# Layer 1 of a graph network on one core: groups written out with constant waits, PSUM operands for DVE, and the next group's scores taken between the adds

## The reference

```
s_u = x @ W_u.T + b_u ;  s_v = x @ W_v.T
e = s_u[src] + s_v[dst];  e = where(e >= 0, e, 0.2 * e)
m = segment_max(e, dst);  e_exp = exp(e - m[dst])
denom = segment_sum(e_exp, dst);  probs = e_exp / denom[dst]
msg = x.reshape(n, 32, 8)[src] * probs[:, None, :]
out = segment_sum(msg, dst)
```

## Time and profile before

| | |
|---|---|
| median of 3 runs | 4665.82 us (4657.55 to 4666.35) |
| profiled execution: its time, its span | 4686.26 us, 4684.5 us |
| busy share of the span: POOL, PE, DVE, ACT | 74%, 66%, 47%, 19% |
| gathers of layer 1 (L1466), 880 | 1039.2 us busy, 326.9 us idle before them |
| products (L1701), 220 | 264.2 us, 1222 ns each |
| adds (L1611), 440 | 188.3 us, 428 ns each |
| matmuls of the pairs (L1532) | 553.5 us |
| mean granted clock of PE | 0.814 |

### The profile page before, as it was taken

How to read it: one execution, slowest core, us unless ns; L and a number is a source line. 1 busy time by engine, 2 the same in 40 slices (tenths; PEclk the granted TensorE clock), 3 DMA queues, 4 the chain that set the end, 5 groups by cost and what they waited for, 6 DMA issues and landing times. The chain is left out here.

```text
span 4684.5 us, 61408 instructions
## 1 busy us (share of the span) xinstructions
PE 3095.6 (66%) x13554; PEld 1900.7 (41%) x13555; DVE 2213.4 (47%) x5019; ACT 908.4 (19%) x2810; POOL 3468.7 (74%) x2948
## 2 busy tenths in 40 slices
PE   2548777877777777777777776884545555555541
PEld 1224444444444444444444443552333333443331
DVE  2553333333333333333333332995766667766665
ACT  0212222222222222222222222332000000000002
POOL 4237888888888888888888886775777777777764
PEclk9768888889888888888889897996777767667765
DMA  8667666667666667666667666565443434444431
GB/s 300 168 235 176 125 132 134 133 126 138 129 133 125 133 131 135 124 133 130 135 125 131 133 133 132 177 202 172 115 113 109 113 113 114 114 112 114 114 102 63
DMA packets 471759, 641.52 MB, mean 137 GB/s; under 512 B 173607, under 2 KB 365635, under 8 KB 467886
## 3 DMA queue, kind: packets, MB, share of 16 engines
q0 software_dynamic: 198144, 339.26, 38.1%
q1 hardware_dynamic: 245994, 254.83, 18.2%
q10 hardware_dynamic: 27588, 47.08, 3.1%
HBM read 448.23 MB, written 192.71 MB: 137 GB/s over the span
## 5 line engine op out<-in xcount | busy, mean ns | idle before, releaser
L935 POOL DMA_INDIRECT S<-l_msum,l_sink x784 | 1284.8, 1639 | 254.2 <-issue 213.0
L1466 POOL DMA_INDIRECT l_feats<-X_rows,l_gsrc x880 | 1039.2, 1181 | 326.9 <-issue 264.6
L918 POOL DMA_INDIRECT l_ga<-A_rows,l_gsrc x784 | 789.7, 1007 | 265.6 <-issue 160.0
L1008 PE MATMUL l_psU<-l_hid,l_same 128*128 128x257 f32 x1568 | 585.9, 459 | 535.6 <-ACT l_hid L1044 505.3
L981 PE MATMUL l_psC<-l_table,l_onehot 128*128 x4728 | 727.4, 295 | 0.0
L1532 PE MATMUL l_psU<-l_feats,l_same 128*128 128x264 f32 x1760 | 553.5, 478 | 169.5 <-DVE l_feats L1701 124.6
L1048 ACT COPY l_msum<-l_psU 128x257 f32<-128x257 f32 x784 | 292.6, 373 | 1889.9 <-POOLq L934 1313.6
L974 PE MATMUL l_psC<-W1cT,l_attrT 64*128 64x256 f32 x1576 | 623.4, 479 | 13.0 <-DMA l_table<-B_rows 13.0
L981 PEld LDWEIGHTS l_psC<-l_table,l_onehot 128*128 128x128 bf16 x4728 | 426.1, 104 | 367.9 <-issue 306.0
L1008 PEld LDWEIGHTS l_psU<-l_hid,l_same 128*128 128x128 f32 x1568 | 267.4, 214 | 666.2 <-ACT l_hid L1044 579.0
L1532 PEld LDWEIGHTS l_psU<-l_feats,l_same 128*128 128x128 f32 x1760 | 409.0, 240 | 306.9 <-issue 216.8
(11 more groups left out here) (346 smaller groups left out, 3390.7 us busy)
## 6 DMA issues: line engine op xcount, KB each, us to landing
l_srcb<-src_rows SPq DMA_DIRECT2D x99, 512.0 KB
l_locb<-lo_rows SPq DMA_DIRECT2D x55, 512.0 KB
S<-su_zeros ACTq DMA_DIRECT2D x24, 1156.5 KB
l_locb<-loc_rows SPq DMA_DIRECT2D x99, 256.0 KB
nd_sums<-S SPq DMA_DIRECT2D x196, 128.5 KB, 2.2
l_attr<-in_edge_attr SPq DMA_DIRECT2D x98, 256.0 KB
GH_rows<-l_hidden SPq DMA_DIRECT2D x49, 384.0 KB
nd_hidden<-GH_rows SPq DMA_DIRECT2D x49, 384.0 KB, 3.1
```

What stands on the lines that cost most here:

```text
L918: pool.indirect_dma_start(ga[:, s, :], None, D["A"], bass.IndirectOffsetOnAxis(ap=gsrc[h][:, j % HALF:j % HALF + 1], axis=0)).then_inc(gat ...
L935: pool.indirect_dma_start(D[f"S{j % NTAB}"], bass.IndirectOffsetOnAxis(ap=sink[j // HALF][:, j % HALF:j % HALF + 1], axis=0), msum[:, j % ...
L1008: nc.tensor.matmul(psU[j % 2][:, 0:UW], same[j // HALF][:, j % HALF, :], hid[:, j % RING, :], start=True, stop=True).then_inc(agg_done, 1)
L1466: pool.indirect_dma_start(feats[r][:, t, :], None, D["X1"], bass.IndirectOffsetOnAxis(ap=gsrc[r][:, t:t + 1], axis=0)).then_inc(gathered[r ...
```

## The change

It does five things, all in layer 1. All 55 groups are written out, on every engine, with constants in the waits in place of register values. A constant row of lane numbers is copied once into a new PSUM bank `psW`, and `find_edge` compares from there. ACT takes the exponential twice: first into `psW`, from where the four products read the weights, then into the gathered rows as before, where PE needs them for the denominators (`weights_in_rows`, for which PE now waits). DVE takes the next group's scores right behind the fourth product, then adds 4 and 5, the local maximum, and adds 6 and 7. PE turns the next group's scores between pairs 5 and 6.

```
+        psW = m.ps("psW", [P, 512])
+        weight = psW[:, 0:GROUP * NH].rearrange("p (t h) -> p t h", h=NH)
+        column = psW[:, P:2 * P]
         def groups(engine, body):
-            body(0, 0, True, False)
-            body(1, 1, False, False)
-            with engine.Fori(1, (XG - 3) // SETS) as u:
-                for r in range(SETS):
-                    body(u * SETS + r, r, False, False)
-            for g in range(XG - 3, XG):
-                body(g, g % SETS, False, g == XG - 1)
+            for g in range(XG):
+                body(g, g % SETS, g == 0, g == XG - 1)
         def ahead(engine, body):
-            with engine.Fori(0, (XG - SETS) // SETS) as u:
-                for r in range(SETS):
-                    body(u * SETS + r, r)
-            body(XG - SETS - 1, 0)
+            for g in range(XG - SETS):
+                body(g, g % SETS)
 # PE
                 pe.wait_ge(same_ready, g + 1)
+                pe.wait_ge(weights_in_rows, g + 1)
                 for n in range(PAIRS):
...
                     i.then_inc(agg_done, 1)
+                    if n == 5 and not last:
+                        turn_scores(g + 1, 1 - r)
                 if not last:
-                    turn_scores(g + 1, 1 - r)
                     gather_ends(g + 1)
 # ACT
                 act.wait_ge(below_ready, g + 1)
-                nc.scalar.activation(feats[r][:, :, H:XW], below[:, :, :], ACT.Exp).then_inc(weights_ready, 1)
+                nc.scalar.activation(weight, below[:, :, :], ACT.Exp).then_inc(weights_ready, 1)
+                nc.scalar.activation(feats[r][:, :, H:XW], below[:, :, :], ACT.Exp).then_inc(weights_in_rows, 1)
 # DVE
-                nc.vector.tensor_tensor(same[:, :, :], K["column"][:, :].unsqueeze(1).to_broadcast([P, GROUP, P]),
+                nc.vector.tensor_tensor(same[:, :, :], column.unsqueeze(1).to_broadcast([P, GROUP, P]),
...
+            nc.vector.tensor_copy(column, K["column"][:, :])
...
-                    f = feats[r][:, q * QUARTER:(q + 1) * QUARTER, :]
-                    f3 = f[:, :, 0:H].rearrange("p t (c h) -> p t c h", h=NH)
-                    w3 = f[:, :, H:XW].unsqueeze(2).to_broadcast([P, QUARTER, H // NH, NH])
+                    f3 = feats[r][:, q * QUARTER:(q + 1) * QUARTER, 0:H].rearrange("p t (c h) -> p t c h", h=NH)
+                    w3 = weight[:, q * QUARTER:(q + 1) * QUARTER, :].unsqueeze(2).to_broadcast([P, QUARTER, H // NH, NH])
...
                 blocks = pair_words(g, 1)
-                add_sums(g, (4, 5, 6, 7), blocks)
                 if not last:
                     take_scores(g + 1, 1 - r, c)
+                add_sums(g, (4, 5), blocks)
+                if not last:
                     local_max(g + 1, 1 - r, c)
+                add_sums(g, (6, 7), blocks)
```

More of the change, by code:

```diff
@@ L1401, in layer1_phase @@
         max_ready, max_turned = m.sem("max_ready"), m.sem("max_turned")
-        below_ready, weights_ready = m.sem("below_ready"), m.sem("weights_ready")
+        below_ready, weights_ready, weights_in_rows = m.sem("below_ready"), m.sem("weights_ready"), m.sem("weights_in_rows")
         weighted, agg_done, acc_done = m.sem("weighted"), m.sem("agg_done"), m.sem("acc_done")
```

## The result

The changed kernel takes 4,922.55 us (median of 4 runs, 4,915.93 to 4,928.98) against 4,664.96 us (median of 4, 4,657.55 to 4,666.35) for the kernel before: ratio 1.0553, interval 1.0540 to 1.0567. It is 5.5% slower where I had forecast 2.7% faster. The profiled execution of the changed kernel took 4,918.33 us around a span of 4,916.6 us.

The account below looks back on a forecast made before the run. GpSimd's gathers were taken to bound each layer 1 group at 23.85 us; afterwards the DVE and PE chain at 21.5. Saving 2.35 us times 54 = 127 us from 4,665.8 gave 4,539, stated as 4538 us, range 4,480 to 4,631.

Parts of the forecast that it names:

- What binds before: Layer 1's groups: GpSimd, full with 16 gathers, sets the 23.85 us period; the DVE and PE chain lies close behind.
- Freed gathers: GpSimd in layer 1: PSUM operands end the gathers' stalls, 3.45 us per group; mean gather 0.96 to 0.98 us.
- Chain 21.5, GpSimd 20.4: the chain binds.: Layer 1's group period after the change: the DVE and PE chain sets 21.5 us, against GpSimd's 20.4.
- The order: DVE and PE, fourth product's end to the next group's L1665: 6.92 us becomes 5.8, including the constant-wait saving of 0.25.
- Constant waits: Written-out groups of layer 1: no register arithmetic before linked instructions, 0.35 us less per group, bounds 0.2 and 0.6.
- The rivals: Layer 1 alternatives: GpSimd as floor (0.12), pairs 6 and 7 at lower clock (0.12), gathers not freed (0.06), slower case (0.05).
- code loading: Rival: written-out groups of layer 1 stall engines fetching new code; period 25.9 us, 111 us slower, 4,777 us; chance 0.05.

Follow-up runs that it names:

- order_only: The kernel before with the new order of scores, adds and transposes alone, operands in SBUF, loops kept: 4,712 us, ratio 1.0115.
- b_all_out: The kernel before with every engine written out and constant waits, nothing else of the change: 4,696 us, ratio 0.9982.
- pause_16: The changed kernel with eight 128x320 memsets on GpSimd in one lump behind the sixteen gathers of each group: 4,905 us, ratio 1.0515.

## Why the prediction was wrong

- **What binds before: right as far as it went.** GpSimd is full, and the comparison and products make it so. The runs that leave both their two SBUF operands have gathers of 1.16 to 1.19 us.
- **Freed gathers: right.** 0.960 us on the mean and none near 2.4, inside the 0.96 to 0.98 that I had named. Comparison and products kept their durations, 2.27 and 1.216 us against 2.28 and 1.222. The two cycle figures of the Trainium skill that I had weighed there (VectorE: DVE Perf Modes, the TRN2 errata) would have made them longer for a PSUM source; these runs do not show it.
- **The failed step: "Chain 21.5, GpSimd 20.4: the chain binds."** The chain was made from hand-overs as long as in the kernel before, where the gathers ran without a delay for 4.0 us at the median and 14.3 at most (from 3,300 to 4,540 us). I took their stall for a pure cost, and put a late signal at nothing. Without the stall the gathers go in an unbroken row of 20 us, and what PE has done inside the second half of that row is seen by DVE and ACT 5 us late at the median, mostly twice per group. If the 6.7 us of new waits are simply taken off, the period is 28.74 - 6.7 = 22.0 us, the upper end that I had given for the chain. That is arithmetic and no run has it: the terms that I had counted for the order and for constant waits were not found, so that the sum comes out may be luck.
- **The order: mechanism seen, value wrong.** The scores follow the fourth product directly (3912.37 + 1.21 against 3913.51), and adds 6 and 7 hardly wait for PE (0.12 and 0.29 us on the mean of all groups). Yet the runs give it no worth: 1.15% slower alone, 0.5% slower with paced gathers. Two things in order_only's trace could be the reason, and no run separates them. The scores are taken earlier, and DVE waits 54.4 us for gathers where it waited 32.7 in the kernel before. And the two hand-overs cost 113.9 us instead of 50.5, in part charged to the transfers of the setup: some late signals are there already.
- **Constant waits: no measurable gain** (0.9982, interval 0.9946 to 1.0017). I had put 0.35 us per group on them, 19 us or 0.4%, which this interval does not exclude; the period of b_all_out, 24.75 us, does not speak for it.
- **The rivals.** The one on the slower side was code loading. Its sign was right and its mechanism wrong: written out everywhere, the kernel before is as fast as in loops. None of my rivals had the freed GpSimd itself as the cause.

**What stays open.** Shown is that late signals come with unbroken rows of freed gathers, whatever the operands, the order and the form of the code, and that breaks every one or four gathers end them. Not shown is through what the gathers act on PE's signals. It may be GpSimd's issuing or the transfers that it starts: in every run the two go together, and none was made that has the one without the other. Nor is GpSimd's own waiting excluded altogether: in pause_16, as in every run with late signals, GpSimd gets ahead and waits too, since the late signals lengthen the period; against it stand only the place where the lateness begins and the memsets under which it ends.

## What to carry to other kernels

An engine that is held up by another may be what keeps the rest prompt: before a stall is taken away, ask what the freed engine will then do without a break, and for how long. Where a wait is charged to a transfer that ended long before, compare the producer's end with the consumer's start directly; a hand-over of some microseconds is a finding of its own. And undo the parts of a change one at a time: here the part with the largest forecast gain made all of the loss.

## What the runs showed of the hardware

- In long unbroken rows of indirect gathers, one every 1.25 us, PE's completions reach DVE and ACT late. In the changed kernel it is nearly all of those due 10.5 us or more into the row, by 5 us at the median and up to 8. In 44 of 55 groups the reader started 2.4 to 2.9 us behind the end of the row's last gather. DVE's completions reached PE in 0.05 to 0.06 us in the same rows.
- At 1.50 us from gather to gather, or with a pause behind every fourth, this is gone; at 1.39 us (128x192) and 1.33 us (128x128) it is there in part.
- A reduction with its one operand in SBUF leaves a gather at 0.960 us, as an operation with one operand in PSUM does; operations with two SBUF operands hold it for up to 2.45 us.
- GpSimd runs a memset of one column between two gathers at no cost in their spacing: 1.25 us with and without it (the kernel with it has the ratio 1.0650 all the same, against 1.0553).
